# A graph layer's first stage with its one-hot rows three blocks ahead, another order of preparation, and a last stage on three engines

## What is computed

```python
# layer 0: mean of x[dst] over the edges of each src, then a linear layer
agg = segment_sum(x[dst], src) / (segment_sum(1, src) + 1e-6)
x = layernorm(x + relu(concat([x, agg], 1) @ W + b))
# layer 1: edge attributes; self loops get the mean attribute of the node
loop_attr = segment_sum(edge_attr, dst) / max(count, 1)
x_l, x_r, e = x @ W_l + b_l, x @ W_r + b_r, edge_attr_and_loops @ W_e
alpha = einsum(leaky_relu(x_l[src] + x_r[dst] + e), att)
out = segment_sum(x_l[src] * softmax_over_dst(alpha), dst) + bias
x = layernorm(x + out)
```

## Time and profile before

| what | value |
|---|---|
| runs | 1611.48, 1605.3, 1601.24 us, median 1605.3 us |
| the profiled execution | 1606.48 us, with a span of 1604.5 us |
| preparation, to the first scatter | 0 to 58.9 us |
| loop of `layer0` (114 blocks) | 58.9 to 757 us |
| last 27 gathers of `layer0` | 757 to 807 us |
| `nodes` and `attend` | 807 to 1559 us |
| `finish` | 1559 to 1604.5 us |
| busy share of the span | PE 74%, PEld 67%, DVE 65%, POOL 59%, ACT 51% |
| mean granted PE clock | 0.913 |

### The profile page before, as it was taken

One profiled execution on the slowest core, in us unless ns is written; L12 is line 12 of the kernel. 1 busy time (PEld: TensorE's weight loads), 2 busy tenths in 40 slices (PEclk: granted clock), 3 DMA queues, 4 the chain that ended last, 5 costly groups with the idle time before them and its releaser, 6 DMA issues. The chain is left out here.

```text
span 1604.5 us, 33129 instructions
## 1 busy us (share of the span) xinstructions
PE 1193.2 (74%) x8732; PEld 1067.5 (67%) x8741; DVE 1043.0 (65%) x2389; ACT 815.2 (51%) x2163; POOL 951.3 (59%) x950
## 2 busy tenths in 40 slices
PE   4666677788788777777799678888878888888650
PEld 2555666677677766666676567777877787777640
DVE  6321123565556565555665469888988888888858
ACT  1354445545545445554734566666666566666411
POOL 3366566666666657676000477777777777777501
PEclk9897779999989999999999789999999999999865
DMA  2222224535544445454400343333333333333101
GB/s 67 76 89 82 76 71 146 153 118 151 151 126 148 129 132 156 148 155 127 130 1 26 87 124 102 97 98 100 102 98 97 98 100 99 93 103 90 27 1 40
DMA packets 177436, 160.94 MB, mean 100 GB/s; under 512 B 23337, under 2 KB 145023, under 8 KB 177261
## 3 DMA queue, kind: packets, MB, share of 16 engines
q1 hardware_dynamic: 148076, 100.82, 21.7%
q0 software_dynamic: 29184, 58.01, 12.1%
HBM read 127.10 MB, written 34.39 MB: 101 GB/s over the span
## 5 line engine op out<-in xcount | busy, mean ns | idle before, releaser
L1194 POOL DMA_INDIRECT xl<-xl_rows,src_idx x456 | 465.4, 1021 | 282.6 <-POOLq L937 144.0
L400 POOL DMA_INDIRECT sorted_rows<-row,place_idx x456 | 457.7, 1004 | 285.3 <-issue 234.6
L635 DVE TENSOR_TENSOR attr_sum<-attr_sum,ps_a 128x516 f32 x114 | 78.7, 690 | 224.2 <-PE ps_a L847 221.1
L1470 PE MATMUL ps_cs<-w_e,attr_t 128*125 128x128 f32 x912 | 190.3, 293 | 2.7 <-DVE work_c L1384 2.7
L1471 PE MATMUL ps_cs<-src_sum,onehot_ct 128*125 x912 | 189.0, 292 | 0.0
L809 PE MATMUL ps_t<-ident,onehot 125*128 125x125 f32 x456 | 81.5, 307 | 129.1 <-ACT onehot L432 108.3
L478 ACT COPY row<-ps_x 125x512 f32<-125x512 f32 x114 | 66.7, 585 | 204.9 <-PE ps_x L854 203.5
L641 DVE TENSOR_TENSOR src_sum<-src_sum,ps_g 128x516 f32 x122 | 84.0, 688 | 121.8 <-PE ps_g L823 121.8
L809 PEld LDWEIGHTS ps_t<-ident,onehot 125*128 125x128 f32 x456 | 54.9, 155 | 155.1 <-ACT onehot L432 131.6
L1470 PEld LDWEIGHTS ps_cs<-w_e,attr_t 128*125 128x125 f32 x912 | 151.7, 208 | 3.1 <-issue 2.6
L426 ACT ACTIVATE apart<-column,dst_lo 125x128 f32<-125x128 f32 x456 | 145.5, 392 | 10.6 <-DVEq L577 10.6
(11 more groups left out here) (322 smaller groups left out, 2396.1 us busy)
## 6 DMA issues: line engine op xcount, KB each, us to landing
row_in<-sorted_rows SPq DMA_DIRECT2D x135, 264.0 KB, 3.2
attr<-in_ea SPq DMA_DIRECT2D x456, 62.5 KB
attr_c<-in_ea SPq DMA_DIRECT2D x456, 62.5 KB
sorted_rows<-row,place_idx POOLq DMA_INDIRECT x456
xl<-xl_rows,src_idx POOLq DMA_INDIRECT x456, 3.5
xl_rows<-x_nodes SPq DMA_DIRECT2D x5, 320.0 KB, 2.5
out<-x SPq DMA_DIRECT2D x4, 320.0 KB
sorted_rows<-x SPq DMA_DIRECT2D x5, 66.0 KB, 2.0
```

What stands on the lines that cost most here:

```text
L400: pool.indirect_dma_start(out=m.sorted_rows.rearrange("p k w -> (p k) w"), out_offset=bass.IndirectOffsetOnAxis(ap=m.place_idx[:, k:k + 1] ...
L1194: pool.indirect_dma_start(out=xl[off % RING][:, u, :], out_offset=None, in_=m.xl_rows, in_offset=bass.IndirectOffsetOnAxis(ap=m.src_idx[:, ...
L1470: pe.matmul(out, attr_t[off % 2][:, u, :], m.w_e[:], start=True, stop=False)
```

## The change

In `layer0`:

- **Step order.** PE: spread(j), turn(j+1), attribute sums(j), gathers, phase work. ACT: copy of row(j), copy_turned(j+1), make_onehot(j+3); step 0 makes two. The ring of one-hot rows stays three.
- **Phases.** 17 instead of 14. `find_totals` is cut into five pieces of five matmuls, one in a step. `find_ends` comes first. PE and DVE take their share of a chunk, of the counts and of the window in the same step. The first pairs of part 0 move into steps 0 and 1. Work of `FIRST_AT` moves from step 78 to 84 and is spread over more steps.
- **Preparation.** The clearing of `src_sum` and `attr_sum` and the setting of the six `row` buffers go from POOL to ACT (`fill`). DVE finds the ends of slots and the tile numbers before the chunks, and gives `tiles_ready` for SP's loads there; `pick` is multiplied in five pieces; PE turns block 0 before the last chunk.

In `finish`: POOL also adds `x1` to the self loop; DVE adds once, reduces, and no longer subtracts the mean, reduces squares or multiplies by the root; ACT squares node tile by node tile with the mean as bias and the sum accumulated (25 instructions), and writes the output as scale times row plus shift (25 more).

The diff, cut:

```diff
-PHASES = ("buckets", "totals", "starts", "first pair", "pairs", "chunk 1", "chunk 2", "chunk 3", "chunk 4", "place", "window",
-          "placed", "picked", "stored")
+PHASES = ("buckets", "ends", "totals 0", "totals 1", "totals 2", "totals 3", "totals 4", "totals", "counts", "chunk 0", "chunk 1",
+          "chunk 2", "chunk 3", "chunk 4", "place", "places", "window")
...
-            sp.wait_ge(numbers_ready, 1)
+            sp.wait_ge(tiles_ready, 1)
...
-            pool.memset(m.src_sum[:], 0.0).then_inc(src_added, 1)
-            pool.memset(m.attr_sum[:], 0.0).then_inc(attr_added, 1)
             for b in range(B):
                 pool.memset(attr[b][:, :, P:P + 1], 1.0).then_inc(preset, 1)
-                pool.memset(row[b][:], 1.0).then_inc(preset, 1)
...
+            fill(m.src_sum[:], (g.NT + U - 1) * (P + 1), 0.0).then_inc(src_added, 1)
             copy_totals(0)
+            for b in range(B):
+                fill(row[b][:], U * ROWW, 1.0).then_inc(rows_set, 1)
+            fill(m.attr_sum[:], (g.NT + U - 1) * (P + 1), 0.0).then_inc(attr_added, 1)
...
             for j in steps:
-                if j + 1 < NB:
-                    copy_turned(j + 1)
                 if j < NB:
                     act.wait_ge(spread_done, j + 1)
...
-                if j + 2 < NB:
-                    act.wait_ge(dst_ready, min(((j + 2) * U + U - 1) // CR, NP - 1) + 1)
-                    make_onehot(j + 2)
+                if j + 1 < NB:
+                    copy_turned(j + 1)
+                for k in ((2, 3) if j == 0 else (j + 3,)):
+                    if k < NB:
+                        act.wait_ge(dst_ready, min((k * U + U - 1) // CR, NP - 1) + 1)
+                        make_onehot(k)
...
+            find_ends(0)
             step.inc(dve.tensor_scalar(m.node_i[:], node_of[0:1, :], float(NT - 1), None, ALU.min))
             link(dve.tensor_tensor(t_of[:], iota_k[0:1, :], node_of[0:1, :], ALU.subtract))
-            find_ends(0)
-            for c in range(5):
-                place_chunk(0, c, CHUNK_BANKS[c])
+            dve.tensor_copy(m.tile_i[:], t_of[:]).then_inc(tiles_ready, 1)
+            place_chunk(0, 0, CHUNK_BANKS[0])
...
+                if j < NB:
+                    pe.wait_ge(turned_copied, j + 1)
+                    if j >= 1:
+                        pe.wait_ge(row_copied, j)
+                    for u in range(U):
+                        mm = pe.matmul(ps_x[0:TE, u * P:(u + 1) * P], onehot_t[j % 2][:, u, :],
+                                       m.x[:, bass.ds(nodes_of[j][u], 1), :], start=True, stop=True)
+                    mm.then_inc(spread_done, 1)
                 if j + 1 < NB:
                     turn(j + 1)
...
-                    find_totals(p)
+                    find_ends(p)
+                for c in range(5):
+                    if (p := phase_at.get((j, f"totals {c}"))) is not None:
+                        find_totals(p, range(c * NT // 5, (c + 1) * NT // 5))
...
                 for c in range(5):
-                    if (p := phase_at.get((j + 1, PHASES[4 + c]))) is not None:
+                    if (p := phase_at.get((j, PHASES[CHUNK0 + c]))) is not None:
                         pe.wait_ge(chunk_placed, 5 * p + c)
-                        pe.wait_ge(placed, p)
+                        pe.wait_ge(dst_ready, p + 1)
                         sum_chunk(p, c, ps_c)
...
+                link(dve.tensor_tensor(y, m.x[:, chunk(c), :], sums[:, chunk(c), 0:D], ALU.add))
+                link(dve.tensor_reduce(mean[:, chunk(c)], y, AX.X, ALU.add))
+                dve.tensor_scalar(mean[:, chunk(c)], mean[:, chunk(c)], -1.0 / D, None, ALU.mult).then_inc(centered, 1)
...
+                weigh(pool, x, 1, c).then_inc(weighed, 1)
+                pool.wait_ge(weighed, c + 1)
+                pool.tensor_tensor(x, x, x1, ALU.add).then_inc(loop_ready, 1)
...
+                for n in range(c * CH, (c + 1) * CH):
+                    act.activation(square[:, n, :], m.x1[:, n, :], ACT.Square, bias=mean[:, n:n + 1],
+                                   accum_out=var[:, n:n + 1]).then_inc(squared, 1)
...
+                    act.activation(m.x1[:, n, :], m.x1[:, n, :], ACT.Identity, bias=shift[:, n:n + 1],
+                                   scale=rstd[:, n:n + 1]).then_inc(out_ready, 1)
```

More of the change, by code:

```diff
@@ L489, in _ @@
                     copy_totals(p)
-                if (p := phase_at.get((j, "window"))) is not None:
+                if (p := phase_at.get((j, "places"))) is not None:
                     copy_places(p)
@@ L495, in _ @@
                 for which in range(2):
-                    if j == FIRST_AT + 2 + which:
+                    if j == FIRST_AT + 3 + 2 * which:
                         act.wait_ge(ends_found, which + 1)
@@ L681, in _ @@
                     find_buckets(p)
-                if (p := phase_at.get((j, "starts"))) is not None:
+                if (p := phase_at.get((j, "ends"))) is not None:
+                    find_ends(p)
+                if (p := phase_at.get((j, "counts"))) is not None:
                     find_starts(p)
-                if (p := phase_at.get((j, "first pair"))) is not None:
+                if (p := 0 if j == 0 else phase_at.get((j, "chunk 0"))) is not None:
                     find_first_pairs(p)
-                if (p := phase_at.get((j, "pairs"))) is not None:
+                if (p := 0 if j == 1 else phase_at.get((j, "chunk 1"))) is not None:
                     find_pairs(p)
                 for c in range(5):
-                    if (p := phase_at.get((j, PHASES[4 + c]))) is not None:
+                    if (p := phase_at.get((j, PHASES[CHUNK0 + c]))) is not None:
                         place_chunk(p, c, ps_c)
-                if (p := phase_at.get((j, "placed"))) is not None:
-                    find_ends(p)
-                if (p := phase_at.get((j, "stored"))) is not None:
+                if (p := phase_at.get((j, "window"))) is not None:
                     place_window(p)
@@ L709, in _, with find_totals @@
         def _(pe):
-            def find_totals(p):
+            def find_totals(p, some):
                 pe.wait_ge(in_bucket_ready, p + 1)
@@ L826, in sum_src @@
                 mm.then_inc(src_summed, 1)
+            pe.wait_ge(preset, COUNTED)
+            pe.wait_ge(buckets_ready, 1)
+            for c in range(CC):
+                mm = pe.transpose(ps_p[0:TE, c * CR:(c + 1) * CR], bucket_f[:, c, :], m.ident[0:CR, 0:CR])
+            mm.then_inc(buckets_turned, 1)
+            pe.wait_ge(buckets_copied, 1)
+            find_totals(0, range(NT))
+            pe.wait_ge(upto_ready, CC)
+            out = ps_a[:, 0:2, :].rearrange("p a w -> p (a w)")
+            for c in range(CC):
+                mm = pe.matmul(out[:, 0:K], ones_half[0:CR, :], upto[:, c, :], start=(c == 0), stop=(c == CC - 1))
+            mm.then_inc(nodes_found, 1)
+            find_counts(0)
+            find_ends(0)
+            for c in range(5):
+                if c == 3:
+                    pe.wait_ge(dst_ready, 1)
+                if c == 4:
+                    pe.wait_ge(chunk_placed, 2)
+                    turn(0)
+                sum_chunk(0, c, CHUNK_BANKS[c])
+            turn_places(0)
+            pick_places(0)
             pe.wait_ge(weights_in, 16 * 11)
@@ L831, in _ @@
             pe.wait_ge(numbers_ready, 1)
-            turn(0)
             nodes_of, places_of, places2, tiles2 = {}, {}, {}, {}
@@ L865, in _ @@
                 if (p := phase_at.get((j, "buckets"))) is not None:
-                    find_totals(p)
-                if (p := phase_at.get((j, "totals"))) is not None:
+                    find_ends(p)
+                for c in range(5):
+                    if (p := phase_at.get((j, f"totals {c}"))) is not None:
+                        find_totals(p, range(c * NT // 5, (c + 1) * NT // 5))
+                if (p := phase_at.get((j, "counts"))) is not None:
                     find_counts(p)
-                if (p := phase_at.get((j, "starts"))) is not None:
+                if (p := 0 if j == 0 else phase_at.get((j, "chunk 0"))) is not None:
                     turn_starts(p)
-                if (p := phase_at.get((j, "first pair"))) is not None:
+                if (p := 0 if j == 1 else phase_at.get((j, "chunk 1"))) is not None:
                     count_pairs(p)
                 for c in range(5):
-                    if (p := phase_at.get((j + 1, PHASES[4 + c]))) is not None:
+                    if (p := phase_at.get((j, PHASES[CHUNK0 + c]))) is not None:
                         pe.wait_ge(chunk_placed, 5 * p + c)
-                        pe.wait_ge(placed, p)
+                        pe.wait_ge(dst_ready, p + 1)
                         sum_chunk(p, c, ps_c)
@@ L889, in _ @@
                 for which in range(2):
-                    if j == FIRST_AT + 1 + which:
+                    if j == FIRST_AT + 2 + 2 * which:
                         pe.wait_ge((first_copied, ends_copied)[which], 1)
```

148 lines of the change are left out of this document (67 added, 81 removed).

## The result

The kernel after took 1500.5 us (median of 4 runs, 1496.5 to 1505.0) against 1605.3 us before: ratio 0.935, 95% interval 0.933 to 0.938. The forecast was 1511, its range 1474 to 1556. The profiled execution has a span of 1503.0 us; before it was 1604.5.

The account below looks back on a forecast made before the run. Waits bound the kernel, in the loop a PE-ACT ring of 5.15 us a block with POOL close behind at 5.22. Loop 67, preparation 20 and `finish` 7 sum to 94 us off, forecast 1511, range 1474 to 1556.

Parts of the forecast that it names:

- The order opens the ring: Loop of `layer0`: spread first ends the 5.15 us cycle of PE and ACT waiting for each other; loop 631 against 698.
- a lead of full buffers: Loop: up to six `row` buffers filled ahead of POOL; PE's side may lose 20 us before POOL starves.
- The first gather of a part: Loop: it waits for its scatters, the load and DVE's rows; estimated 6 us (3 to 9).
- PE's step: Loop: 3.6 us with one gather, 4.3 with register loads in the open, 6.5 with a second gather.
- Registers: PE's register loads, no longer covered by the 1.40 us wait: 0.46 + 0.25 us a step.
- DVE's lateness in the phases: Phase steps with gathers: DVE's queued work delays PE about 1.05 us more per delayed gather; in all 6.15 us a step.
- The preparation: Ahead of the loop: `ident` freed of POOL's memsets, loads earlier; first scatter at 39, gain 20 us (12 to 23).
- `finish`, 7 us: Last stage: DVE's large operations per chunk fall from 7 to 3; gain 7 us, 5 if accumulation costs 0.2.
- The change doesn't do what it says: Rival: in the loop the row copy still waits; only preparation and `finish` gain: 1578 us, chance 0.07.
- POOL throughout: Rival: POOL bounds the whole loop, register loads hidden and DVE's lateness small: 1474 us, chance 0.20.
- DVE's lateness and the registers eat all: Rival: where gathers run, blocks 32 to 113 keep their 492 us: 1545 us, chance 0.23.
- The clock fell: Rival: PE's granted clock falls in blocks 32 to 113; at 0.70 the time is 1659 us, chance 0.05.

Follow-up runs that it names:

- e4: Kernel after with the gathers planned three steps later (7 steps after their part is sorted in place of 4): 1492.7 us.
- e7: Kernel after with the 24 registers PE loads every third step for spread and attribute sums replaced by the constant 0, so wrong windows are used: 1478.9 us.
- e9: Kernel after with VectorE's share of each rank piece one step later than TensorE's, as it was before: 1501.0 us.
- e1: Kernel before with only the order edited: TensorE spreads rows first in a step and ScalarE copies them first: 1514.2 us.
- e6: Kernel after with the memsets of the two sums and the six row buffers back on POOL: 1504.9 us.
- e10: Kernel after with the old step order on both engines: spread last, turned rows copied first, one-hot rows two ahead: 1598.3 us.
- e12: Kernel after with gathers three steps later and TensorE's registers loaded 8 at a time, per block and per gather, in place of 24: 1480.6 us.
- e11: Kernel after with gathers three steps later and TensorE's 24 registers loaded behind the attribute sums of the step before: 1511.8 us.

## Why the prediction held

The total was 10 us too high, and its sum of 94 stands against 101.5 us in the profiled executions (about 76.6 in the loop, 18.7 ahead of it, 6.5 in `finish`). But its parts were less right than the total.

- **The order opens the ring, POOL paces, and a lead of full buffers covers PE.** Right. Blocks 0 to 21: 121 forecast, 116.4 measured; 22 to 31: 52 and 53.0; 32 to 42: 57 and 58.7; 43 to 63: 120 and 117.4. POOL's 5.22 us a block were 5.3 there. That the lead would be used up near block 53 was right too (1.6 us at block 54).
- **The first gather of a part, 6 us (3 to 9).** It cost the row side 14.6 us at step 32 (185.2 to 204.9 between two row copies, 19.7 us, in which POOL needs 5.1), of which 8.21 are the wait for the load and some 3.5 the lower clock behind it. The forecast left 20 us of lead behind this step; 9.8 were left. That the lead at block 43 and its end near block 54 came out right all the same is luck: I let blocks 32 to 42 use 12 us of it, and they used 2, since PE's steps there were shorter than my 6.15 us. e4 shows what the lost lead was worth: 8 us of time for one number.
- **PE's step.** One gather: 3.6 forecast, 3.54 measured. The add of 0.90 before a second gather stands as forecast (25.3 us in 29 waits). Registers: 0.71 us a step was too much, 0.33 measured (14.9 + 4.9 us over 60 steps); I take it that not each set of loads comes when PE's queue is empty. e7 fits the sum of what shows: its loop is 20.4 us shorter. It leaves out only the loads of the spread and of the attribute sums, yet the 4.9 us ahead of the gathers are gone with them (0.2 us of "issue" left over blocks 54 to 113), so these were not the price of the gathers' loads alone.
- **DVE's lateness in the phases, 1.05 us for each chunk, with it 6.15 us a step.** The mis-sized term. Blocks 64 to 84 took 120.1 us and not 129, 5.72 a step. e9 moved DVE's share and changed nothing: DVE's time then shows at another wait. The one large case of it was outside the phases, `slot_flags` (DVE's step 90, PE's wait in step 91), with 5.0 us of PE's wait for `attr_sum`; blocks 85 to 113 took 156.0 where 152 was forecast.
- **The preparation, 20 us.** The mechanism and the places were right (`ident` 0.29, first scatter at 40.17 for 39). As a term that adds to the loop's gain it was wrong: a later start does not move the end by as much. e1, whose first scatter comes 13.6 us later than in after, ends its loop 4 us later; e6's delay of 6.7 us arrives in part or not at all; under the old order 17 us arrive not at all (e10). The loop's own gain was put too low: 67 forecast, 76.6 measured, and 86.3 in e1 by the order alone. So no run shows that the new phases help the loop; e1's old ones stood in a loop 9.7 us shorter, which can be its later start.
- **`finish`, 7 us, or 5 if the accumulation costs 0.2.** The gain is 6.5. A second instruction of 0.19 us stands behind each of the 25 squares, but it overlaps with its neighbours: the next square starts 0.40 us after the last (1475.09 - 1474.69), where the five scaled rows without accumulation take 2.03, or 0.41 each. Both are above my 0.32, but ACT has the time, since the chunks come from POOL and DVE more slowly (`L1619` and `L1564` took 17.2 us in ten operations, 16 forecast). The estimate by the Trainium skill's rule of the exclusive lock ("SBUF — State Buffer", "SBUF: two separate sides"), at worst 2.45 us for a DVE operation beside POOL and a gain of 3, was not met: of DVE's ten large operations with two inputs four were held and took 1.77 to 2.04 us, and six took 0.81 or 0.82. (The prediction speaks of two more places where the trace agrees with the rule, and names one.)
- **The rivals.** "The change doesn't do what it says", 1578, was built as e10 and gave 1598: the preparation does not add to a closed ring as I had summed it. "POOL throughout", 1474, needed the registers hidden and the lead kept; with both done, e12 gives 1480.6. "DVE's lateness and the registers eat all", 1545, counted what my 6.15 us a step counted, and with the lead used up the steps took 5.72. The clock fell in blocks 22 to 31 (0.74), where PE had 25 us of lead, and cost nothing.

## What to carry to other kernels

Where a step's time equals the time of the next engine, ask not what the step takes but what lead it lets build: before, the usual step took 5.15 us against POOL's 5.1 (four times 0.97 and 0.30), and still 77 us lay in the loop, since the lead was 1.3 to 1.6 us nearly throughout and every longer step was paid in full. Two ways to open one ring are worth little more than one, and a gain ahead of a loop need not arrive at its end: take it as a term only where a trace shows the same engine pacing from there to the end. A stretch that ends at one engine's last instruction can look shorter because another's work has moved behind it (e4): look at the end of that work too. Small per-step control work (registers) belongs in every step in small portions, not in a block every third step.

## What the runs showed of the hardware that I had not expected

- Loads of 24 registers on PE show as waits up to 1.7 us, two such sets in a row as 3.3 us, and loading them behind queued matmuls hid none of it (e11). Sets of 8 show 0.5 us at most and mostly nothing (e12).
- PE's clock: behind a pause of 3.07 us eight matmuls still took 1.09 us, and behind 0.90 more the next eight took 1.93, at a granted clock of 0.50 (e11); after 6.56 us of wait at step 32 they took 2.08. After 0.90 alone, such eight took 1.06 (e12, at 341.64).
- An ACT activation with an accumulated sum is followed by a second instruction of 0.19 us, which overlaps: five such pairs and five scaled rows without a sum both take some 0.4 us each.
